# A third pair buffer, one adjacency row buffer, an earlier read of finished ring rows and earlier q passes in a four-layer graph attention kernel

## What is computed

```python
# layers 0 and 1: scores are a sum of a row term and a column term
e = leaky_relu(s_src[:, :, None] + s_dst[:, None, :]);  attn = softmax(where(adj > 0, e, NEG))
h_prime = elu(attn @ h)
# layer 2: eight heads
scores = einsum('bmhd,bnhd->bhmn', q, k) / 8 + edge_bias[adj]
attn = softmax(where(adj > 0, leaky_relu(scores), -1e9));  out = concat(attn @ v) @ Wp + bp
# layer 3: additive attention over 64 features, for each pair (i, j)
s = leaky_relu(u[:, :, None, :] + v[:, None, :, :]);  e = einsum('bijf,f->bij', s, a)
attn = softmax(where(adj > 0, e, NEG));  h_prime = elu(attn @ hp)
```

## Time and profile before

| what | value |
|---|---|
| median of 3 runs | 9574.74 us (9552.55 to 9577.66) |
| the profiled execution's own time | 9553.52 us |
| its span, first to last instruction | 9551.7 us |
| busy: PE, DVE, ACT, POOL | 8058.2, 7573.2, 7327.1, 1494.0 us (84, 79, 77, 16%) |
| mean granted TensorE clock | 0.952 |
| the 2560 moves of pairs, median from issue to landing | 4.7 us |

### The profile page before, as it was taken

How to read it: one execution, slowest core, us unless ns; L and a number is a source line. 1 busy time by engine, 2 the same in 40 slices (tenths; PEclk the granted TensorE clock), 3 DMA queues, 4 the chain that set the end, 5 groups by cost and what they waited for, 6 DMA issues and landing times.

```text
span 9551.7 us, 176152 instructions
## 1 busy us (share of the span) xinstructions
PE 8058.2 (84%) x64968; PEld 3662.9 (38%) x64968; DVE 7573.2 (79%) x10983; ACT 7327.1 (77%) x8541; POOL 1494.0 (16%) x582
## 2 busy tenths in 40 slices
PE   5788888888888888888888888888888888888888
PEld 3434343343433434334343343433434334343432
DVE  5687877878778787887878878788787887878878
ACT  3587777878778787787877878778787777878877
POOL 0301203012030210302103030030301203012000
PEclk8899999999999999999999999999999999999999
DMA  3525244352443524335243352533425244353430
GB/s 96 133 65 117 72 97 99 74 124 67 100 95 77 124 67 100 91 80 125 57 109 91 79 121 54 115 83 87 114 62 121 73 97 102 73 118 73 99 75 19
DMA packets 519920, 864.97 MB, mean 91 GB/s; under 512 B 91938, under 2 KB 157474, under 8 KB 518946
## 3 DMA queue, kind: packets, MB, share of 16 engines
q1 hardware_dynamic: 518946, 852.41, 38.4%
HBM read 76.25 MB, written 4.19 MB: 8 GB/s over the span
## 4 chain that ended last, share of the span: by engine, by line
PE 37%; DVE 30%; issue 16%; DMA 8%; SPq 4%; ACT 4%; DVEq 1%; POOL 0%; ACTq 0%; POOLq 0%
PE psum L875 16%; DVE work L1463 15%; DMA work<-work 8%; PE psum L748 6%; PE psum L786 6%; DVE work L1273 5%; SPq L538 4%; DVE work L1301 3%; PE psum L744 3%; ACT work L1126 2%; PE psum L767 2%; PE psum L679 1%; DVE probs L1414 1%; ACT work L984 1%; ACT work L993 1%
## 5 line engine op out<-in xcount | busy, mean ns | idle before, releaser
L875 PE MATMUL psum<-work,pick 128*32 128x512 f32 x32768 | 4025.8, 620 | 489.9 <-DVE top L1414 249.5
L1126 ACT ACTIVATE work<-v,ucol 128x1024 f32<-128x1024 f32 x3627 | 3928.8, 1141 | 640.5 <-PE psum L875 639.4
L1463 DVE TENSOR_SCALAR work<-v,ucol 128x1024 f32<-128x1024 f32 x4565 | 3446.6, 809 | 518.5 <-PE psum L875 433.5
L1301 DVE STREAM_TRANSPOSE work<-work 128x1024 f32<-128x1024 f32 x1280 | 1584.2, 1238 | 781.8 <-DMA work<-work 780.8
L984 ACT ACTIVATE work<-psum,beta 128x1024 f32<-128x1024 f32 x1024 | 1139.5, 1113 | 1149.4 <-PE psum L748 676.0
L875 PEld LDWEIGHTS psum<-work,pick 128*32 128x32 f32 x32768 | 960.2, 112 | 2763.5 <-issue 2318.9
L1273 DVE CUSTOM_DVE_ANT_0 work<-psum,work 128x1024 f32<-128x1024 f32 x1280 | 1535.6, 1200 | 404.8 <-ACT work L984 394.6
L993 ACT ACTIVATE work<-work,least 128x1024 f32<-128x1024 f32 x1280 | 1465.4, 1145 | 34.0 <-DVE least L1273 33.8
L744 PE MATMUL psum<-mask_next,ident_b 128*128 128x512 bf16 x2560 | 814.4, 401 | 797.1 <-DVE least L1273 599.2
L786 PE MATMUL psum<-work,vw 128*64 128x128 f32 x16384 | 1141.1, 282 | 18.5 <-DMA work<-work 18.5
L786 PEld LDWEIGHTS psum<-work,vw 128*64 128x64 f32 x16384 | 897.6, 139 | 667.7 <-issue 651.7
(11 more groups left out here) (158 smaller groups left out, 5053.7 us busy)
## 6 DMA issues: line engine op xcount, KB each, us to landing
work<-work SPq DMA_DIRECT2D x2560, 256.0 KB, 4.7
adj_in<-in_adj SPq DMA_DIRECT2D x128, 512.0 KB, 5.0
tile3T<-blocks SPq DMA_DIRECT2D x512, 128.0 KB, 2.7
mask<-mask_next SPq DMA_DIRECT2D x128, 256.0 KB, 2.7
x_in<-in_x SPq DMA_DIRECT2D x16, 256.0 KB, 4.8
xT_both<-in_xT SPq DMA_DIRECT2D x16, 256.0 KB, 5.9
out<-yout SPq DMA_DIRECT2D x16, 256.0 KB, 2.6
work<-in_WqT SPq DMA_DIRECT2D x1, 128.0 KB
```

Of the source, the lines that this page charges most:

```text
L875: mm = pe.matmul(score3[32 * q:32 * q + 32, cols], pick[:, 15 - kk:47 - kk], ring[u % RING][q][:, cols], start=(kk == 0), stop=(kk == 15), ...
L1126: ins = act.activation(ring[u % RING][q], v3[:], ACT.Relu, bias=ucol[:, 4 * T + q, kk:kk + 1])
L1301: dve.transpose(dst[:, :, :, m % 2, :], by_part(probs[m % 3])).then_inc(s_blocks, 1)
L1463: ins = dve.tensor_scalar(ring[u % RING][q], v3[:], ucol[:, 4 * T + q, kk:kk + 1], 0.0, ALU.add, ALU.max)
```

## The change

It does the following.

1. `pairT` gets a third buffer, `work` grows by two rows of 4 KB for it. In layer 2 pair k uses buffer (k - 8) mod 3, in layers 0 and 1 it stays k mod 2. In layer 2 a move from pair 11 on waits for the product of pair k - 3. Pair 10's waits for GpSimd's `acc` (`s_acc`), since `xdup` now lies in the third buffer.
2. `adj_in` keeps one row tile in place of two. Each load waits until the tile just before it has been read. `ADJ_AT` goes from slots 110, 112, 128, 131, 134, 140, 147, 156 to 110, 128, 132, 137, 142, 146, 150, 156. The first graph's loads follow the same rule.
3. `TOP3_AT` is one slot earlier, and `last_top` comes first in VectorE's slot, ahead of tiles and units.
4. `make_q` for heads 2 to 7 stands ahead of the slot's ring step; `q_high` and `q_low` come one slot after it, not two.
5. `ACT_UNIT`, `DVE_UNIT` go from 1.07, 0.69 to 1.1, 0.76. With the moved side work, ScalarE's units of a body rise from 228 to 236 of 512, and in the last graph from 207 to 217.

```diff
-ACT_LAG, DVE_LAG = 2, 2
+ACT_LAG, DVE_LAG, Q_LAG = 2, 2, 1
+def pair_buffer(k):
+    return k % 2 if k < PAIRS_A else (k - PAIRS_A) % 3
-TOP3_AT = {STEPS.index(16 * T) + 1: T for T in range(NT)}
+TOP3_AT = {STEPS.index(16 * T): T for T in range(NT)}
-ADJ_AT = {110: 0, 112: 1, 128: 2, 131: 3, 134: 4, 140: 5, 147: 6, 156: 7}
+ADJ_AT = {110: 0, 128: 1, 132: 2, 137: 3, 142: 4, 146: 5, 150: 6, 156: 7}
-ACT_UNIT, DVE_UNIT, PE_STEP = 1.07, 0.69, 1.72
+ACT_UNIT, DVE_UNIT, PE_STEP = 1.1, 0.76, 1.72
-        adj_in = sb("adj_in", [P, 2, N], I32)
+        adj_in = sb("adj_in", [P, N], I32)
-        work = sb("work", [P, 23, N])
+        work = sb("work", [P, 25, N])
-        pairT = [two_of(19), two_of(21)]
+        pairT = [two_of(19), two_of(21), two_of(23)]
+        xdup = work[:, 23, :].rearrange("p (t k f) -> p t k f", t=NT, k=2)
@@ next_adj
-                ready(s_adj_free, a * NT + t - 1)
+                ready(s_adj_free, a * NT + t)
@@ move_pair
-                if k >= 2:
-                    ready(s_pv, a * PAIRS + k - 1)
+                if k == PAIRS_A + 2:
+                    ready(s_acc, a * HP + 1)
+                elif k >= 2:
+                    ready(s_pv, a * PAIRS + (k - 1 if k < PAIRS_A + 2 else k - 2))
@@ first graph's loads
-            load_adj(0, 1)
-            for t in range(2, NT):
-                sp.wait_ge(s_adj_free, t - 1)
+            for t in range(1, NT):
+                sp.wait_ge(s_adj_free, t)
                 load_adj(0, t)
@@ TensorE, layer3
                     if more and s in TILE_AT:
                         scores(g + 1, it, TILE_AT[s])
+                    if more and s in Q_AT:
+                        make_q(g + 1, it, Q_AT[s])
@@ ScalarE and VectorE, ahead
-                if s - ACT_LAG in Q_AT:
-                    q_high(it, Q_AT[s - ACT_LAG])
+                if s - Q_LAG in Q_AT:
+                    q_high(it, Q_AT[s - Q_LAG])
-                if s - DVE_LAG in Q_AT:
-                    q_low(a, it, Q_AT[s - DVE_LAG])
+                if s - Q_LAG in Q_AT:
+                    q_low(a, it, Q_AT[s - Q_LAG])
@@ VectorE, slots
-                    if g is not None and kk is None:
+                    if g is not None:
                         last_top(g, s, tail)
                     if a is not None:
                         tiles(a, it, s, flagged)
                     if g is not None and kk is not None:
                         if STEPS[s] + 1 < GROUPS:
                             ring_units(g, STEPS[s] + 1, a is not None)
-                        last_top(g, s, tail)
```

More of the change, by code:

```diff
@@ L138, in uses_of @@
             uses.append(("a", TILE_AT[s]))
+        if ahead and s in Q_AT:
+            uses.append(("q", Q_AT[s]))
         if ring:
@@ L168, in uses_of @@
                 uses.append(("vw", 0))
-            if s in Q_AT:
-                uses.append(("q", Q_AT[s]))
             if s in VW_AT:
@@ L253, in side_work @@
         pe += {17: 1.0, 24: 1.0, 26: 1.8, 27: 1.8, 28: 1.8 * layer, 29: 1.8 * layer}.get(v, 0.0)
-    act += (1.0 if s - ACT_LAG in Q_AT else 0.0) + (1.0 if s - 2 in VW_AT else 0.0) + (0.6 if s in COPY_AT else 0.0)
-    dve += (1.2 if s - DVE_LAG in Q_AT else 0.0) + (1.4 if s - 2 in HEADS_AT else 0.0)
+    act += (1.0 if s - Q_LAG in Q_AT else 0.0) + (1.0 if s - 2 in VW_AT else 0.0) + (0.6 if s in COPY_AT else 0.0)
+    dve += (1.2 if s - Q_LAG in Q_AT else 0.0) + (1.4 if s - 2 in HEADS_AT else 0.0)
     dve += {END_2 + 13: 2.8, END_2 + 14: 3.0, END_2 + 17: 0.8, TOP_ALL_AT: 0.1}.get(s, 0.0) + (1.2 if s in TOP_AT else 0.0)
@@ L320, in build @@
         x_in = sb("x_in", [P, NT, F])
-        xdup = sb("xdup", [P, NT, 2, F])
         x_split = sb("x_split", [P, N], F32R)
@@ L527, in load_adj @@
             def load_adj(a, t):
-                sp.dma_start(adj_in[:, t % 2, :],
+                sp.dma_start(adj_in[:],
                              adj[bass.ds(a, 1), t * P:(t + 1) * P, :].rearrange("a p j -> p (a j)")).then_inc(s_adj[t % 2], 16)
             def next_adj(a, t):
-                ready(s_adj_free, a * NT + t - 1)
+                ready(s_adj_free, a * NT + t)
                 load_adj(a, t)
@@ L542, in move_pair @@
                 ready(s_blocks, a * TILES + 2 * k + 2)
-                if k >= 2:
-                    ready(s_pv, a * PAIRS + k - 1)
+                if k == PAIRS_A + 2:
+                    ready(s_acc, a * HP + 1)
+                elif k >= 2:
+                    ready(s_pv, a * PAIRS + (k - 1 if k < PAIRS_A + 2 else k - 2))
                 elif not_first(a):
                     ready(s_pv, a * PAIRS)
-                move(pairT[k % 2].rearrange("p (i y) -> p i y", i=4), blocks[k % 2], s_moved[k % 8])
+                move(pairT[pair_buffer(k)].rearrange("p (i y) -> p i y", i=4), blocks[k % 2], s_moved[k % 8])
             def move_tile(g, T, it, used):
@@ L762, in pv_pair @@
                 pair_arrived(a, k)
-                src = pairT[k % 2].rearrange("p (a b t i) -> p b a t i", a=4, t=2, i=32)
+                src = pairT[pair_buffer(k)].rearrange("p (a b t i) -> p b a t i", a=4, t=2, i=32)
                 for j in range(NT):
@@ L781, in pv_heads @@
                     pair_arrived(a, k)
-                src = pairT[k % 2].rearrange("p (a b h i) -> p b a h i", a=4, h=2, i=32)
+                src = pairT[pair_buffer(k)].rearrange("p (a b h i) -> p b a h i", a=4, h=2, i=32)
                 for j in range(half * NT // 2, (half + 1) * NT // 2):
@@ L938, in _ @@
                     scores(0, first, TILE_AT[s])
+                if s in Q_AT:
+                    make_q(0, first, Q_AT[s])
                 ahead(0, first, s)
@@ L1231, in _ @@
                 dve.wait_ge(s_adj[t % 2], (t // 2 + 1) * 16)
-                dve.tensor_scalar(codes, adj_in[:, t % 2, :], float(TYPES - 1), CODE, ALU.min, ALU.mult)
-                dve.tensor_scalar(no_edge[:], adj_in[:, t % 2, :], 0.0, MASKED, ALU.is_le, ALU.mult)\
+                dve.tensor_scalar(codes, adj_in[:], float(TYPES - 1), CODE, ALU.min, ALU.mult)
+                dve.tensor_scalar(no_edge[:], adj_in[:], 0.0, MASKED, ALU.is_le, ALU.mult)\
                    .then_inc(s_adj_free, 1)
@@ L1582, in convert @@
                 ready(freed(it, used), uses_before(it, used) + 1)
-                pool.tensor_scalar(mask_next[:, t, :], adj_in[:, t % 2, :], float(TYPES - 1), CODE, ALU.min, ALU.mult)
-                pool.tensor_scalar(no_edge[:], adj_in[:, t % 2, :], 0.0, MASKED, ALU.is_le, ALU.mult)\
+                pool.tensor_scalar(mask_next[:, t, :], adj_in[:], float(TYPES - 1), CODE, ALU.min, ALU.mult)
+                pool.tensor_scalar(no_edge[:], adj_in[:], 0.0, MASKED, ALU.is_le, ALU.mult)\
                     .then_inc(s_adj_free, 1)
```

2 lines of the change are left out of this document (removed).

## The result

The median after is 8736.11 us (8734.80 to 8738.61, 4 runs); the ratio to before is 0.9129, 95% interval [0.9113, 0.9145]. The gain is 838 us, about twice the 429 of the forecast, and the time lies outside its range. The profiled execution has a span of 8733.7 us, 818.0 less than before.

The account below looks back on a forecast made before the run. Waits bound the kernel, chiefly layer 2's loop of product, move, turn and scores. 27.5 us a body over 15 bodies, 412, with first-graph and last-graph terms made 429 saved: 9145 us forecast, range 8990 to 9410.

Parts of the forecast that it names:

- The mechanism: Layer 2: the pair buffer holds a ready move about 8 us until an earlier product ends, stalling VectorE, then TensorE.
- the stall stays: Rival, 7%: `blocks` still has two buffers, so half the layer 2 stalls stay; 9350 us.
- SyncE is held: Rival, 5%, slower: adjacency loads waiting for conversions delay layer 2 moves queued behind them on SyncE; 9685 us.
- nothing changes: Rival, 5%: gains of 6 and costs of 6 us, about 9575 us.
- supply takes over: Rival, 19%: in layer 2 ScalarE and VectorE are late in place of the move, TensorE at 89%; 9335 us.
- the ceiling on TensorE: Layer 2: of 38.4 us a body, 27 taken with TensorE at 91% busy; bounds 21 and 38.
- the clock: Layer 2: TensorE runs about 2.5 us at half rate after each of five long gaps, 5 us a body.
- Part 4: Finished rows read first: half of 10 us of TensorE's waits go, 5 us a body; bounds -4 and 10.
- part 3: q one slot earlier: gain counted within the 11.8 us of q waits; delayed ring steps cost nothing, bounds 0 and 2.
- The planner: New unit costs: eight of 512 units move to ScalarE, taken as 0 us; bounds -2 and 2.
- The costs of part 2: One adjacency buffer: 3 us VectorE contention and 1.5 us late deviation a body, plus 15 us once for first-graph loads.
- all of it is gained: Rival, 10%: layer 2 gives 31 to 33 us, the reads 8, costs 2, so 38 a body; 8990 us.

Follow-up runs that it names:

- e2_old_wait: The changed kernel with three pair buffers, but each layer 2 move waits for pair k - 2's product as before; 9359.9 us, ratio 0.9788.
- e8_filler: The kernel before plus three zero-weight products ahead of the scores of eight layer 2 slots, nothing taken away; 9442.78 us, ratio 0.9872.
- e3_top_late: The changed kernel with the read of finished rows back at its old place and slot; 8882.22 us, ratio 0.9287.
- e4_q_late: The changed kernel with q's product behind the ring step and its passes two slots behind, as before; 8862.63 us, ratio 0.9274.
- e1_buffers_only: The kernel before with only the third pair buffer and the single adjacency buffer; 8913.94 us, ratio 0.9321.
- e5_old_units: The changed kernel with the planner's old unit costs, 1.07 and 0.69; 8763.37 us, ratio 0.9158.
- e6_adj_only: The kernel before with only the single adjacency buffer, its new load slots and stricter wait; 9612.62 us, ratio 1.0045.

## Why the prediction was wrong in size

**The mechanism was right.** The move's wait for the product of pair k - 2 was the bound: `e2_old_wait` shows that nothing else in the change frees it. The rivals that the stall stays, that SyncE is held, and that nothing changes are out. So is the one in which supply takes over: VectorE's wait for ScalarE is 292.1 us in after and 394.6 in before, so it did not grow.

**The step that failed first: the ceiling on TensorE.** The forecast had 38.4 us of waits and clock in layer 2 and took 27, since three coupled engines ran at 89 to 93% in a dense stretch. The measured 45.6 us (301.8 to 256.2) are 33.5 of idle time and 12.1 of busy time. The waits had been summed to 21.6 + 11.8 = 33.4, and all of them went. TensorE runs at 95% where 91 was taken. The 89% of layer 1 was not a ceiling for layer 2: there VectorE was itself at 93%, here it is at 90 (232.76 of 260.00), and ScalarE at 89. The prediction saw that difference and let it count for only two points. The rule it weighed here, that matmul busy share does not tell headroom, is from the Trainium skill's page Perfetto Trace Analysis, Identifying the Most-Contended Engine. The trace does not decide it: the share went past the dense stretch's 89%, and ended at the 95% that the forecast had as its bound without hidden headroom.

**The second: the clock.** The forecast took 2.5 us at the lower level behind each of five gaps, 5 us of time a body. By the granted clock's records, before spent 471 us at it in the layer 2 of the 15 bodies, 31 us a body, and after 48, or 3.2. Half of the 28 us between is 14, and TensorE's busy time there fell by 12.1. The two rows were read rightly, but one gap was taken for the pattern: before has 108 stretches at the lower level in these layers 2, seven a body and 4.4 us each, where five of 2.5 were taken. That is 7 us a body more than the forecast's 5, 106 in all. `e8_filler` agrees on the price, with VectorE's stalls left in place. The Trainium skill's page TensorE: Matmul & The Clock Gate, HAM oscillation, describes this for a kernel that waits for DMA: waits between short bursts of products make each burst start at the lower clock, and the remedy is an order that keeps the engine busy. The trace agrees, here with waits for VectorE: 909 us at the lower level before and 429 after.

**Read and q: the third.** Part 4 was taken at 5 us a body, 75 in all, and 4 in the last graph; part 3 as no gain beyond the 11.8. Taken back from the change (`e3_top_late`), the read is worth 8.8 us a body and 11.0 in the last graph. On top of the buffers, each without the other, they give 51 us (the read, `e4_q_late` against `e1_buffers_only`) and 32 (q, `e3_top_late`), both with the new unit costs; together 178. The forecast had no term for the two together. It had costed the read by TensorE's waits alone, of which 178 us went, more than the 150 that it called possible. The cost feared, units that VectorE used to make ahead, shows in full against `e3_top_late`: 98 us more of waits for ring units (110.6 to 208.4), against 203 less for the read. That the waits for q stand behind the stalls was right by two thirds: 184.7 us in before and 58.2 in `e1_buffers_only`. The last third went only with part 3.

**The planner, 0 forecast:** 30 us, all of its bound of 2 a body. The forecast weighed ScalarE as being as busy as VectorE. By the starts of the ring steps a body of `e5_old_units` lasts 2.1 us more than one of after: 1.2 ahead of layer 2 (211.4 against 210.2), 0.6 behind it (68.7 against 68.1) and none in it. So it is not the stretch with the conversions alone; why the units gain ahead of layer 2 stays open.

**The costs of part 2: too high in the bodies, too low in the first graph.** It took 4.5 us a body and 15 once, 82; measured are 43. Of these the first graph has more than 15: its loads cost what was said (15.5), but the late inverse deviation adds 14.5, which the forecast weighed for the bodies alone. So the other parts gained more there, too: the net of 15.3 us stands on some 42, not on the 28 of the sum. In a body `e6_adj_only` shows 3.1 us behind layer 2 for the 3 + 1.5. Of these, 3.0 may be the clock: time at the lower level there rises from 73 to 162 us in all, and half of it is 45. It also shows 2.7 gained in layer 2, from where two conversions have left, and the sum had nothing for that. In a body of after the deviation is in time:

```profile
4154.39 2.62 POOL L1610 TENSOR_TENSOR rstd<-rstd,neg_half 128x8 f32<-128x8 f32 x1
...
4157.05 1.60 DVE L1347 TENSOR_TENSOR za<-zb,rstd 128x256 f32<-128x256 f32 x2
```

VectorE uses it 0.04 us after it is there, with no wait in brackets: the 1.5 us taken for it did not come. Over the run VectorE waits 22.3 us for it, 18.3 of them in the first graph. The moved contention is real, 23 units at 1099 ns in the mean. SyncE was not held: VectorE's whole wait for moves in the run is 56.2 us. By the Trainium skill, page GPSIMD Engine Reference, Specifications, GpSimd shares its SBUF interfaces with VectorE, and they contend while VectorE is in a two-port mode or reads two inputs from SBUF. The eight slow units fit that; no row shows in which mode a unit runs.

**The sum.** Layer 2 18.6 us a body above the 27 (45.6 less 27), and outside it 7.0 gained (52.6 less 45.6) where 0.5 was forecast (5 - 3 - 1.5): together 25.1 more a body, 376 us. With the last graph (14.6 for 4) and the first (15 for 13) it is 389, the difference between 818 and 429.

**The ranges.** The rival "all of it is gained" had the right form and 10%, but took 31 to 33 us for layer 2, below even its own sum of 38.4, where 45.6 came. The upper bound was the sum of the waits and 5 us of clock, and the clock alone gave 12.1. (The sums of the rivals and of the low end come out 2 to 3 us below the 9335, 9350 and 8990 that the prediction prints, which changes nothing.)

## What to carry to other kernels

Where a wait of an engine sits in a loop with a transfer, sum all of the waits that follow from it and look for a reason in that stage, not in another one, before you discount the sum. Read TensorE's time at the lower clock stage by stage, from all of its records and not from one gap, and count half of it with the waits that cause it. Where a stage runs once without the work that hides its waits, as the first graph here, cost the change there by itself. Two edits that both reorder one engine's list are to be tried together and singly, since one may only repair the other.

## What the runs showed of the hardware that was not expected

- Added work made the kernel 1.3% faster: 24 products a body (8 places, 2.76 us in the one shown) against 283 us less at the lower clock level.
- Ring units of VectorE take 1099 ns in the mean beside GpSimd's conversions and 743 without, but unevenly: the median is 744, and the longest, 2619 ns, began inside an addition of GpSimd and ended just behind it. And GpSimd's conversion slowed too, from the 3802 ns of the earlier trace rows to 3927 in a kernel where VectorE is busy 87% of the time instead of 79:

```profile
L1590 POOL TENSOR_SCALAR mask_next<-adj_in 128x1024 bf16<-128x1024 int32 x120 | 471.2, 3927 | 1306.9 <-DVE least L1281 591.5
```
